# Finer steps in VectorE's generators and new order lists for three engines in a vision tower on one core

## What is computed

```
h = concat(cls, patches @ W.T)                        # 32 x 37 x 192
x = LN(LN(h));  k, v, r = x @ Wk.T, x @ Wv.T, sigmoid(x @ Wr.T)
y = bi_wkv(decay, first, k, v)                        # scan in both directions over the 37 tokens
x = LN(h) + r * y @ Wo.T
x = x + sigmoid(LN(x) @ Wrf.T) * (relu(LN(x) @ Wkf.T)**2 @ Wvf.T)
h = h + x
z = LN(h);  scores = sigmoid(z @ router + b);  top 2 of 4 groups, top 4 of 16 experts, weights w
h = h + sum_e w_e * (silu(z @ Wg_e) * (z @ Wu_e)) @ Wd_e + shared expert
```

## Time and profile before

| | us |
|---|---|
| median of 3 runs | 283.24 |
| runs | 283.08, 283.24, 285.62 |
| profiled execution, span from first to last instruction | 281.7 |
| TensorE busy | 227.2 |
| VectorE busy | 203.3 |
| ScalarE busy | 146.7 |
| GpSimd busy | 17.3 |

### The profile page before, as it was taken

How to read it: one execution, slowest core, us unless ns; L and a number is a source line. 1 busy time by engine, 2 the same in 40 slices (tenths; PEclk the granted TensorE clock), 3 DMA queues, 4 the chain that set the end, 5 groups by cost and what they waited for, 6 DMA issues and landing times.

```text
span 281.7 us, 4262 instructions
## 1 busy us (share of the span) xinstructions
PE 227.2 (81%) x1400; PEld 209.9 (75%) x1400; DVE 203.3 (72%) x502; ACT 146.7 (52%) x300; POOL 17.3 (6%) x25
## 2 busy tenths in 40 slices
PE   1393246418966698799989999999999999999994
PEld 1272146208955598698879999899999999999993
DVE  4459999899699899979988489778532175644443
ACT  3487927885537998537395683422552342212220
POOL 4202001130001000001010000100000010000000
PEclk9999559955899999999999999999999999999999
DMA  5676624000000014400001440000054100004410
GB/s 142 195 253 200 247 76 128 0 2 0 0 0 2 1 22 96 114 0 2 1 2 41 173 138 2 0 5 0 14 180 142 33 2 1 0 4 97 108 32 24
DMA packets 13014, 17.47 MB, mean 62 GB/s; under 512 B 2336, under 2 KB 11074, under 8 KB 12866
## 3 DMA queue, kind: packets, MB, share of 16 engines
q1 hardware_dynamic: 12722, 17.11, 20.1%
q10 hardware_dynamic: 272, 0.11, 0.2%
HBM read 16.22 MB, written 0.99 MB: 61 GB/s over the span
## 4 chain that ended last, share of the span: by engine, by line
PE 54%; DVE 28%; ACT 7%; issue 7%; DMA 2%; POOL 1%; SPq 0%; DVEq 0%; POOLq 0%; ACTq 0%
PE PG L885 14%; PE PA L905 13%; PE PG L887 8%; PE PF L905 5%; DVE S L689 4%; PE PQ L885 3%; DVE mx L662 3%; DVE stats L612 2%; DVE K L710 2%; PE PQ L887 2%; DVE S L694 2%; DMA w_tok<-in_w_tok 2%; DVE stack L640 2%; PE PX L922 1%; PE PG L922 1%
## 5 line engine op out<-in xcount | busy, mean ns | idle before, releaser
L885 PE MATMUL PG<-stack,hi_egu 128*128 128x222 f32 (+1 forms) x288 | 62.2, 324 | 2.1 <-ACT act L541 1.2
L541 ACT ACTIVATE act<-PG,columns 128x222 f32<-128x222 f32 (+3 forms) x56 | 28.3, 506 | 61.9 <-PE PG L887 60.4
L835 DVE SCALAR_TENSOR_TENSOR hid<-PG,columns,act 128x222 f32<-128x222 f32 (+1 forms) x52 | 27.3, 524 | 45.0 <-PE PG L887 33.4
L885 PEld LDWEIGHTS PG<-stack,hi_egu 128*128 128x128 f32 x288 | 44.9, 190 | 6.4 <-DVE hid L835 3.4
L905 PE MATMUL PA<-w_ed,hid 128*124 128x192 f32 (+1 forms) x240 | 46.2, 328 | 2.0 <-DVE hid L844 2.0
L887 PE MATMUL PG<-stack,lo_egu 128*128 128x222 f32 (+1 forms) x192 | 42.7, 304 | 0.0
L905 PEld LDWEIGHTS PA<-w_ed,hid 128*124 128x124 f32 (+1 forms) x240 | 38.2, 183 | 3.5 <-issue 3.2
L887 PEld LDWEIGHTS PG<-stack,lo_egu 128*128 128x128 f32 x192 | 31.7, 190 | 0.0
L372 POOL TENSOR_TENSOR rstd<-var,minus_half 112x2 f32<-112x2 f32 (+3 forms) x12 | 14.3, 1189 | 209.9 <-DVE var L620 209.9
L905 PE MATMUL PF<-w_down,mix_hid 128*124 128x192 f32 (+1 forms) x120 | 24.3, 339 | 0.0
L844 DVE TENSOR_TENSOR hid<-hid,gates 128x222 f32<-128x222 f32 (+1 forms) x48 | 21.4, 463 | 0.7
(11 more groups left out here) (226 smaller groups left out, 401.0 us busy)
## 6 DMA issues: line engine op xcount, KB each, us to landing
gates<-in_w_egu SPq DMA_DIRECT2D x6, 512.0 KB, 3.6
gates<-c_rows SPq DMA_DIRECT2D x16, 138.8 KB, 2.8
gates<-c_rows SPq DMA_DIRECT2D x16, 92.5 KB, 2.7
gates<-c_rows SPq DMA_DIRECT2D x16, 83.2 KB, 2.5
w_ed<-in_w_ed SPq DMA_DIRECT2D x1, 1152.0 KB, 5.8
gates<-c_rows SPq DMA_DIRECT2D x16, 55.5 KB, 2.5
gates<-in_w_up SPq DMA_DIRECT2D x2, 384.0 KB, 3.2
pat<-in_patches SPq DMA_DIRECT2D x2, 370.0 KB, 3.8
```

The lines of the kernel that those rows point to most:

```text
L541: nc.scalar.activation(act[128 - gate:128, n % 2, 0:G.n], PG[0:gate, gate_bank(n), 0:G.n], ACT.Silu, bias=bias).then_inc(act_silu, 1)
L835: V_.scalar_tensor_tensor(out, PG[part, 1, 0:G.n], bias, act[part, i, 0:G.n], ALU.add, ALU.mult).then_inc(mul_done, 1)
L885: mm(out, w_hi[:, slot, cols], x[:, p, 0:G.n], start=(p == 0), stop=False, skip_group_check=True)
```

## The change

The generators of VectorE yield between dependent operations, and a `settle()` moves from in front of a yield to behind it, so that the order list can put other work between an operation and its user. On `var1` one wait inside the pair is dropped: both variances now count on the semaphore that GpSimd waits for. In `dve_gated` the wait for `pe_down` stands ahead of the waits for `act_silu` and `pe_value`. No operation is added or taken out, shapes and tiles are as before, and GpSimd's and SyncE's programs are the same but for the count that `root` waits for. VectorE's list has 390 steps where it had 282. The three lists are written anew.

```diff
-                ("var_ready", 1), ("pool_rstd", 1), ...
+                ("var_ready", (2, 1, 1)), ("pool_rstd", 1), ...
...
-                pool.wait_ge(var_ready[n], at(var_ready[n], g, 1))
+                pool.wait_ge(var_ready[n], at(var_ready[n], g, 2 if n == 1 else 1))
...
+            yield f"stats{n}"
             settle_apart()
             for t in range(G.tiles):
                 step(V_.bn_aggr(mv[0:G.tp, t, :], stats[0:G.tp, t, :]))
+            yield f"aggr{n}"
             settle()
             mean_sq = mv[0:G.tp, 0:G.tiles, 1]
             if n == 1:
-                do(V_.tensor_scalar(var[0:G.tp, 1, 0:G.tiles], mean_sq, 1.0 + EPS, EPS * EPS, ALU.mult, ALU.add))
+                V_.tensor_scalar(var[0:G.tp, 1, 0:G.tiles], mean_sq, 1.0 + EPS, EPS * EPS, ALU.mult, ALU.add).then_inc(var_ready[n], 1)
             V_.tensor_scalar(var[0:G.tp, 0, 0:G.tiles], mean_sq, EPS, None, ALU.add).then_inc(var_ready[n], 1)
+            yield f"var{n}"
...
-            do(V_.tensor_tensor(sums, old_sums(0, wk), old_sums(1, wk), ALU.add))
+            step(V_.tensor_tensor(sums, old_sums(0, wk), old_sums(1, wk), ALU.add))
             yield "sum"
-            do(V_.tensor_tensor(sums, sums, view(mx, OWN, WK, 2, wk), ALU.add))
+            settle()
+            step(V_.tensor_tensor(sums, sums, view(mx, OWN, WK, 2, wk), ALU.add))
             yield "sum2"
...
-            do(V_.tensor_tensor(ahead[rs], other, mine, ALU.subtract))
-            do(V_.tensor_tensor(ahead[rs], ahead[rs], before[0:tp, None, :, :].broadcast_to(G4), ALU.is_gt))
+            step(V_.tensor_tensor(ahead[rs], other, mine, ALU.subtract))
+            yield "apart"
+            settle()
+            step(V_.tensor_tensor(ahead[rs], ahead[rs], before[0:tp, None, :, :].broadcast_to(G4), ALU.is_gt))
+            yield "ahead"
+            settle()
...
-                v.wait_ge(act_silu, at(act_silu, g, n + 1))
-                if n:
-                    v.wait_ge(pe_value, at(pe_value, g, n))
                 if n < 2:
                     since(v, pe_down, g)
...
                     v.wait_ge(pe_down, at(pe_down, g, n - 1))
+                v.wait_ge(act_silu, at(act_silu, g, n + 1))
+                if n:
+                    v.wait_ge(pe_value, at(pe_value, g, n))
...
 PE_ORDER = _order(
-    "F2:tok0 M0:tr2 F2:tok1 F2:tr1a M0:rf M0:up0 M0:up1 M0:mix0 M0:up2 M0:mix1 M0:up3 M0:mix2 M0:up4 M0:mix3 M0:up5 M0:mix4",
+    "M0:tr2 F2:tok0 F2:tok1 M0:rf M0:up0 M0:up1 M0:mix0 M0:up2 M0:mix1 M0:up3 M0:mix2 M0:up4 M0:mix3 M0:up5 M0:mix4 M0:mix5",
```

More of the change, by code:

```diff
@@ L641, in split_low @@
                                  ALU.subtract).then_inc(stack_ready[n], 1)
+                yield f"tr{n}{'ab'[k]}"
         def dve_front(v, g):
@@ L646, in dve_front @@
             step, settle, do, settle_apart = steps
-            moments(v, steps, g, 1, h0[g % 2])
-            yield "var1"
+            yield from moments(v, steps, g, 1, h0[g % 2])
             shift_rows(v, g, 1, 2)
             yield "ln1"
-            split_low(v, g, 1, full[1])
-            yield "tr1"
+            yield from split_low(v, g, 1, full[1])
             def run(x, d):
@@ L671, in dve_front @@
             V_.memset(edge_e1(wk), NEG).then_inc(exp_in, 1)
-            yield "sb"
+            yield "edge"
             settle()
-            do(V_.tensor_tensor(top[:, 0:wk], old_max(0, wk), old_max(1, wk), ALU.max))
+            step(V_.tensor_tensor(top[:, 0:wk], old_max(0, wk), old_max(1, wk), ALU.max))
+            yield "top0"
+            settle()
             v.wait_ge(act_kf, at(act_kf, g, 1))
-            do(V_.tensor_tensor(top[:, 0:wk], mx[:, OWN:OWN + wk], top[:, 0:wk], ALU.max))
-            yield "top"
+            step(V_.tensor_tensor(top[:, 0:wk], mx[:, OWN:OWN + wk], top[:, 0:wk], ALU.max))
+            yield "top1"
+            settle()
             for i, a in enumerate((old_max(0, wk), old_max(1, wk), mx[:, OWN:OWN + wk])):
@@ L711, in dve_front @@
                 yield f"recip{h}"
+            since(v, pe_o, g)
             settle()
-            since(v, pe_o, g)
             V_.tensor_tensor(Zm[:, 0:G.n], K[:, G.blocks[0]], E1[:, WK:WK + G.n], ALU.mult)
@@ L742, in dve_mid @@
             v.wait_ge(x1_ready, at(x1_ready, g, 1))
-            moments(v, steps, g, 2, x1)
-            yield "var2"
+            yield from moments(v, steps, g, 2, x1)
             shift_rows(v, g, 2, 1)
             yield "ln2"
-            split_low(v, g, 2, full[2])
-            yield "tr2"
+            yield from split_low(v, g, 2, full[2])
             v.wait_ge(act_rf, at(act_rf, g, 1))
@@ L756, in dve_mid @@
                 step(V_.scalar_tensor_tensor(gate_r[0:tp, a:b, :], gate_r[0:tp, a:b, :], 1.0, rows(PF, G, bank, a, b), ALU.add, ALU.mult))
+            yield "gated"
             settle()
-            do(V_.scalar_tensor_tensor(h[rs], gate_r[rs], 0.5, base[g % 2][rs], ALU.mult, ALU.add))
+            step(V_.scalar_tensor_tensor(h[rs], gate_r[rs], 0.5, base[g % 2][rs], ALU.mult, ALU.add))
             yield "h1"
-            moments(v, steps, g, 3, h)
-            yield "var3"
+            settle()
+            yield from moments(v, steps, g, 3, h)
             shift_rows(v, g, 3, 1)
             yield "ln3"
-            split_low(v, g, 3, PF)
-            yield "tr3"
+            yield from split_low(v, g, 3, PF)
             v.wait_ge(pe_router, at(pe_router, g, 1))
@@ L768, in dve_mid @@
             parts = PQ[0:tp, 0:tiles * 2 * EXPERTS].rearrange("p (t h e) -> p t h e", h=2, e=EXPERTS)
-            do(V_.tensor_tensor(sc[rs], parts[:, :, 0, :], rbias[0:tp, None, :].broadcast_to(E3), ALU.add))
+            step(V_.tensor_tensor(sc[rs], parts[:, :, 0, :], rbias[0:tp, None, :].broadcast_to(E3), ALU.add))
+            yield "high"
+            settle()
             V_.tensor_tensor(sc[rs], sc[rs], parts[:, :, 1, :], ALU.add).then_inc(logits_ready, 1)
@@ L797, in dve_mid @@
                                   rank[0:tp, 0:tiles, :, None].broadcast_to([tp, tiles, EGROUPS, EPG]), ALU.mult))
+            yield "kept"
             settle_apart()
@@ L808, in dve_mid @@
             settle()
-            do(V_.scalar_tensor_tensor(sc[rs], left[0:tp, 0:tiles, 0:EXPERTS], TAKEN, sc[rs], ALU.is_equal, ALU.mult))
-            do(V_.tensor_reduce(cnt[rs], sc[rs], AXX, ALU.add))
-            do(V_.tensor_scalar(cnt[rs], cnt[rs], 1e-20, None, ALU.add))
-            do(V_.reciprocal(cnt[rs], cnt[rs]))
+            step(V_.scalar_tensor_tensor(sc[rs], left[0:tp, 0:tiles, 0:EXPERTS], TAKEN, sc[rs], ALU.is_equal, ALU.mult))
+            yield "taken"
+            settle()
+            step(V_.tensor_reduce(cnt[rs], sc[rs], AXX, ALU.add))
+            yield "total"
+            settle()
+            step(V_.tensor_scalar(cnt[rs], cnt[rs], 1e-20, None, ALU.add))
+            yield "guard"
+            settle()
+            step(V_.reciprocal(cnt[rs], cnt[rs]))
+            yield "share"
             since(v, pe_cT, g)
+            settle()
             V_.scalar_tensor_tensor(c_pad[0:tp, 0:tiles, CROW:CROW + EXPERTS], sc[rs], SCALE,
```

44 lines of the change are left out of this document (31 added, 13 removed), and 94 rows, old and new, of tables (ACT_ORDER, DVE_ORDER, PE_ORDER).

## The result

| | before | changed kernel |
|---|---|---|
| median, us | 284.06 | 273.96 |
| lowest and highest of 4 runs, us | 283.08, 285.62 | 272.17, 276.29 |
| profiled execution: time, span, us | 281.7 (span) | 274.81, 273.0 |

The ratio is 0.9626, with a 95% interval of 0.9577 to 0.9674: 10.1 us less by the medians, where 276.4 stood against 283.24, 6.8 less. The median lies inside the range given.

The account below looks back on a forecast made before the run. VectorE was taken to set the pace first, TensorE later, so gains come only from TensorE idle ahead of 147.3 us. 138.3 + 135.8 + 0.8 = 274.9 span, plus 1.5 gives 276.4 us; range 271.8 to 283.5.

Parts of the forecast that it names:

- Step 1: Group 0's mid stage moved ahead on TensorE and VectorE: its first unit starts at 75.7 us, 11.8 us earlier.
- I take full clock: At group 0's `rf`, which follows `F2:tok` without a gap, TensorE was assumed to run at full clock.
- the rival: Half clock stays over `rf` and six `up`/`mix` pairs: 4.2 us more, 280.6 us; chance 0.13.
- Step 2: Work between dependent VectorE pairs saves 0.12 us each: 4.6 us, 1.7 ahead of `M0:tr3`, 2.9 behind it.
- the yields give nothing: Rival: parting dependent VectorE pairs saves nothing, 4.6 us more, 281.0 us; chance 0.09.
- Step 3: From group 0's first unit to group 1's: VectorE and TensorE floors plus holes put `G1:g0` at 138.3 us.
- edits at nothing: Weight loads, gate DMAs and `dve_gated` wait order were costed at nothing; gate DMAs under 1 us.
- "in step" rival: VectorE and TensorE in step up to group 1's units: `G1:g0` at 144, 12 us of holes, 282 us; chance 0.15.
- The slower rival: 26 VectorE handovers among S and X steps cost TensorE 0.45 us each: 11.7 more, 288.1 us; chance 0.13.
- Step 4: From group 1's first unit to the end: 135.8 us plus 0.8 for local misfits, span 274.9.

Follow-up runs that it names:

- z_first: Changed kernel with group 1's `sum` to `z` moved back ahead of group 0's `gated` in VectorE's list: 280.17 us, ratio 0.9799 to the kernel before.
- filled_mid: Changed kernel plus 29 filler matmuls around group 0's mid stage (ahead of `F1:r`, `M0:tr2`, `F2:tok1`): 270.58 us, ratio 0.9524 to the kernel before.
- second profile: Profile of the changed kernel timed once more as it is, beside the kernel before: median 273.98 us, ratio 0.9561; profiled span 269.2.
- filled_all: Changed kernel plus 231 filler matmuls at 13 places on TensorE: 268.51 us, ratio 0.945 to the kernel before.
- yields_only: New generators with all three order lists as in the kernel before: 284.65 us, ratio 1.0004 to the kernel before.
- old_then_new: Old lists up to group 0's first unit, then the remaining steps in the new order: 282.74 us, ratio 0.9935 to the kernel before.
- new_then_old: New generators; new lists up to group 0's first unit, then the remaining steps in the old order: 291.14 us, ratio 1.0143 to the kernel before.

## Why the prediction was right, and where it was not

**Step 1, the mid stage ahead: right.** The second split was forecast to end at 54.0 and ended at 53.6; `rf` at 55, measured 55.71 and 54.51. g0 was forecast at 75.7: 74.86 at the high clock, 79.28 at half. The price came too: `z` ends at 83.83 in the first profile and 79.42 in the second (80.7 forecast, at full clock), `hi_k` starts at 90.13 and 85.78 (86.7), and neither made TensorE wait over a microsecond. z_first shows this move to be over half of the gain.

**"I take full clock": wrong in one execution, right in the other.** The reason given, that `rf` follows `F2:tok` without a gap, looked at the wrong gap. In both profiles TensorE had waited twice before it (1.08 and 1.58 us, 1.32 and 1.39, ahead of group 1's `hi_r` and of `M0:tr2`), and the clock fell behind that, at 50.0 and at 49.2 us: the eight `w_tok` products that follow are long in both (2.62 and 2.79 us, and 1.48 in filled_mid, which fills those waits). What differs is when it rose again. In the second profile it was back at 52.6 us, and the four `w_tok` products just ahead of `rf` take 0.92 us; in the first it was back only at 63.6, they take 1.64, and `rf` and the pairs inherited it. So the gaps to look at were those one stage earlier; why the clock came back early in one execution and late in the other, with waits so alike, no run shows. The size of the rival was right: 4.2 forecast, 4.4 at g0 and 3.8 in the span measured. What was missing is that it is not one case or the other but a spread within one kernel's runs, which filled_mid and filled_all take away.

The Trainium skill ("TensorE: Matmul & The Clock Gate", section "Part 1: The HAM clock gate (the \"warmup\" mystery)") says that the time before the clock rises varies from run to run of one kernel, and these profiles agree (52.6 and 63.6 us). It also says that for a model this penalty is under 1% of a typical span, and speaks of one rise at the start of a kernel. Here the clock fell four times in the first profile, and holding it gave 5.5 of 274.0 us by the medians, 2.0%, and 1.1 to 1.8% by the ratios: the measurement decides.

**Step 2, the yields: right in kind, too large.** 4.6 us were forecast ahead of G1, 1.7 of them ahead of g0; with the clock held putting the waits back costs 3.4 and 1.9, and 3.0 of the time. The price of a pair was right where VectorE is the bound: ahead of g0 14 pairs were forecast at 1.7 and gave 1.9. Behind it, where TensorE is nearly full, the term gave 1.5 (3.4 less 1.9) of its 2.9. The rival "the yields give nothing" falls. They are worth nothing, though, without the lists (yields_only). The Trainium skill ("VectorE: DVE Perf Modes", section "The DRAIN you can't avoid") says that a semaphore between two operations "costs nothing extra"; here putting the waits back cost 3.0 us, and the measurement decides.

**Step 3, the stretch up to group 1's units: two errors that cancel.** At full clock 62.6 us were forecast between the marks, 56.3 of TensorE's work and 6.3 of holes. The profiles have 61.35 and 61.44, with 56.94 and 57.03 of work. That looks as if the work had been priced well, and it is luck: over the first 10.7 us of the stretch the clock was 0.61 and 0.60. filled_all, at full clock from 33 us on, shows what that hides. There the marks are 60.11 apart, and TensorE is busy for 55.12, 1.36 of it with fillers: 53.8 of its own. Against the 51.99 before, the moved products added 1.8 us where 4.3 were forecast, and half clock made up the difference. The holes at full clock are 60.1 - 53.8 = 6.3, as forecast (the fillers stand in 1.4 of them); at half clock 4.4 are left, since the stretched products fill some. The "in step" rival (12 us of holes) and the slower one (0.45 us a handover) fell by the same count. Of the edits at nothing, the DMAs of the gates held VectorE once, for 0.8 and 1.0 us, about the 1 us allowed. G1 at 138.3 lies between 136.30 and 140.63, and 133.68 is what the clock assumed for it gives in filled_all.

**Step 4, the rest: the step that was mis-sized.** 135.8 + 0.8 = 136.6 were forecast from G1 on; 132.4 and 132.9 were measured. What was wrong in it is that it kept TensorE's waits as they were. Most are too short to show as idle: I took the earlier trace rows for a TensorE with 4.85 us to lose, most of it tail, and it had more, hidden in its busy time. An estimate from the starts of its matmuls, the sum of what each stands above the median distance for its pair of shapes, gives 11.7 us from G1 to the end before and 9.3 after: 2.4 us of waits less. By the same medians the work that changed sides added 0.8 us, not 1.4. That leaves 0.4 us of the 2.0 without a place. The 0.8 for misfits was not needed.

The distance between the first units of groups 1 and 2, 57.40 before and 55.38 after, with 77.0 behind in both, would put all of the difference in the first part. But group 1's `d13` and group 2's `cT`, 1.2 us of work, ran ahead of group 2's first unit before and run behind it now. So the equal 77.0 hold 1.2 us more work after the change, and waits were saved in both parts. The list behind unit 0 does this, not the early start: old_then_new has it without the early start (55.42), and new_then_old, with the early start and the old list, doesn't (57.60).

**The sum, and what is luck in it.** The time stands 1.8 us above the span in the profiled run (1.5 taken). The forecast of 276.4 was 2.4 above the median, but it was made for full clock. The run that has full clock, filled_all, took 268.51, and the forecast is 7.9 above that: in its profile g0 came 2.1 us sooner than forecast, the stretch between the marks was 2.5 shorter and the rest 4.1. The clock that was not expected gave back over half of the error.

**The slower rival** did not come, but its premise has a form that did: new_then_old shows that the early unit gives a loss when the old order stands behind it. The change is one piece: front half alone +1.4%, back half alone -0.7%, both -4%.

## What to carry to other kernels

When two orders are compared, look for what the moved piece leaves behind it: here the stage brought forward paid only with the steps that follow laid out for its new time. Where TensorE's idle stretches precede a stage on the critical chain, look at its clock in that stage in more than one execution, and try a few matmuls that wait for nothing in front of the waits: here 29 of them took away the longer runs (3.4 us by the medians), and 231 gave more, while in the kernel before 34 of them in the wrong place made VectorE 2.6 us late. When a sum is made for one state of the clock, check it against an execution in that state: a total that fits in another can hide two errors. A place between dependent VectorE operations is worth something only if the order fills it.

## What the runs showed of the hardware

The clock over 50 to 63 us was 0.90 in one execution of a program and 0.50 in another, with TensorE busy for the same 11.88 us. Fillers in an unused PSUM bank held it at 0.99 over the span, and the runs lay within 1 us where they had spread over 8. With the clock held, a VectorE wait ahead of independent work cost 0.14 us each where VectorE set the pace (1.9 us for 14) and 0.07 behind, where TensorE was nearly full.
